# The num group of each retention step runs one step later, beside the den group, with six product tiles instead of four

## The chip, the cores and the metric

The kernel runs on one core of one Trainium2 chip. The metric is the device time of one execution in microseconds; lower is better. The core has five engines that run their own instruction streams in program order and meet through semaphores: TensorE (PE, matmuls), VectorE (DVE), ScalarE (ACT), GpSimd (POOL) and SyncE (SP, which issues the DMAs here). A "launch" is the whole program: eight images, three stages, one after the other.

## The reference

Only the first layer matters for this change. For each of 8 images with 1024 tokens of 256 channels, group-normalised, it computes, for 8 heads of 32 channels:

```
qr = theta_shift(xf @ Wq.T);  kr = theta_shift(xf @ Wk.T * SCALING);  vr = xf @ Wv.T
qk  = einsum('bhqd,bhkd->bhqk', qr, kr) * mask
den = clip(abs(qk).sum(-1), 1.0, 50000.0)
out = einsum('bhqk,bhkd->bhqd', qk / den, vr)
out = gelu(layernorm_per_head(out) * ln_g + ln_b) @ Wo.T;   x = x + out
```

There is no softmax: the weights are the scores times a fixed decay mask, divided by the sum of their absolute values. The kernel sums `num` = products times values and `den` = absolute products times ones apart, and divides later, inside the normalisation. The second layer (causal attention over 1024 tokens, then eight dense experts) follows in two more stages and is not touched.

## The kernel before

**Tiling.** The retention stage (`layer0`) walks each image `b` in 4 phases `p` of 8 steps `kt`, 32 steps in all. A phase is one group of four heads (`g = p // 2`) and one half of the 512 queries (`c = p % 2`); a step is one tile of 128 keys. The first and the last image are written out, the six between them are one loop body (`Fori(1, B - 1)`).

**A step.** Four heads make two pairs `j`. In step `i` TensorE issues, in this order: `scores` of pair 0 of the *next* step into the two-bank PSUM tile `scores0`; the first half of that step's odd job; `scores` of pair 1 of the next step into `scores1`; the second half of the odd job; the **den** group (`sums`) of step `i - 1`; the **num** group (`weighted`) of step `i`. VectorE's `products` multiplies each pair's scores by the mask window (`window`) into one of the `prod` tiles, and so frees the scores bank; ScalarE's `absolutes` takes the absolute value of each `prod` tile into one of four `absp` tiles. `scores` of pair `j` of step `i + 1` waits until `products` of pair `j` of step `i` is done, because there is just one scores tile for each pair. `prod[n % 4]` may be written again when num and the absolute value of two steps before are done.

**Odd jobs.** Between the scores pairs TensorE also does, at fixed steps: the projections for the phases to come (`q` at kt 0, `k` at kt 3, or 5 and 6 in phase 2, `v` at kt 6, or 7 in phase 2) into `bankA`; the transposes of the finished phase, `nT` (`transpose_n`, L285, into `bankB`) and `dT` (`transpose_d`, L291, into `bankA`), both at kt 1; in phase 2 the two tiny group sums `gn1` and `gn2` of the next image (L280, kt 2 and 3); `zT` and the output projections. All jobs in `bankA` stand in the list `A_MID`; each waits (`a_free`) until the one before it has been read. `dT` follows `q`, so it waits until `q` has been read by VectorE's `q_rotate_in` (L464, kt 1). `gn1` follows `dT`, so it waits for VectorE's `take_den` (L510, at kt 3 between the two products).

**Turning the phase.** After the last step of a phase ScalarE copies the sums out: `take_num` (L683, `l_tA<-l_num`) and `take_den` (L687, `l_tB<-l_den`). In step kt 0 of the new phase ScalarE's order is `take_num`, the two `absolutes`, `take_den`.

**The chain through `t1`.** A q or k that was projected is rotated in one set of buffers, `t1`, `t2`, `hi` and `lo`. In phase 3 of each image but the last, k of the next image is still in them: at kt 0, as the last thing of the step, ScalarE makes `hi` of it (`high`, L666), then GpSimd makes `lo` (`low`, L779), and only then may VectorE's `q_rotate_in` (L464) write `t1` again. VectorE runs in order, so `shuffle` (L472), `rotate_sin` (L477) and all products behind it wait with it.

Of the kernel before, what the change touches and what calls it, by code (L numbers as in the profile page):

```python
# [14 lines left out]
ACT = mybir.ActivationFunctionType  # L15
# [5 lines left out]
def layer0(nc, x, xT, wqT, wkT, wvT, woT, lng, lnb, window, rowscale, cosT, sinT, avg8, ident, x1):  # L21
# [7 lines left out]
    B, L, E = x.shape  # L29
    H, HD = 8, E // 8  # L30
    QC = 512
    KT = L // 128
# [3 lines left out]
    LN_EPS, GN_EPS = 1e-5, 1e-5  # L36
    SCALING = float(HD) ** -0.5
    STACK = 12 * 16


    A_HEAD = ["gn1", "gn2", "k", "v", "q", "v'", "k'"]
# [27 lines left out]
    with ExitStack() as ctx:  # L69
# [16 lines left out]
        kst = [sb(f"kst{g}", [128, 4, L], F32R) for g in range(2)]  # L86
        qst = [sb(f"qst{c}", [128, 4, QC], F32R) for c in range(2)]
        vsb = [sb(f"v{g}", [128, KT, 128]) for g in range(2)]
        prod = [sb(f"prod{n}", [128, 2, QC]) for n in range(4)]
        absp = [sb(f"absp{n}", [128, 2, QC]) for n in range(4)]  # L90
        tA, tB = sb("tA", [128, 4, 128]), sb("tB", [128, 4, 128])
        z = sb("z", [128, 2, L])
# [128 lines left out]
        def _(pe):  # L221
# [107 lines left out]
            def weighted(b, i, first):  # L329

                p, kt = i // KT, i % KT
                g = p // 2
                if p % 2 == 0 and kt % 4 == 0:
                    pe.wait_ge(v_ready, 4 * b + 2 * g + kt // 4 + 1)
                if kt == 0 and not (first and p == 0):
                    pe.wait_ge(n_taken, 4 * b + p)
                pe.wait_ge(prod_ready, 2 * STEPS * b + 2 * i + 2)
                for h in range(4):
                    mm = nc.tensor.matmul(num[32 * h:32 * h + 32, :], vsb[g][:, kt, 32 * h:32 * h + 32],  # L339
                                          prod[2 * (i % 2) + h // 2][:, h % 2, :], start=(kt == 0), stop=(kt == KT - 1))  # L340
                mm.then_inc(av_done, 1)

            def sums(b, i, first):
# [27 lines left out]
            def body(b, first, last):  # L371


                def A(name, task, *args):

                    if task not in (project, project_v) or args[-1] != 1:
                        a_free(name, b, first, last)
                    task(*args)

                def Bk(name, task, *args):  # L380
                    if task is not out_proj or args[-1] != 1:
                        b_free(name, b, first, last)
                    task(*args)

                for i in range(STEPS):
                    p, kt = i // KT, i % KT
                    prev = p == 0
                    post = not (prev and first)
                    tag = "3'" if prev else str(p - 1)
                    ph = nphase(b, p - 1, prev)  # L390
                    g, c = ((p + 1) // 2 % 2, (p + 1) % 2)
                    prep_q, prep_kv = p < 3 or not last, p < 2 or not last
                    nb, ni = (b, i + 1) if i + 1 < STEPS else (b + 1, 0)
                    more = i + 1 < STEPS or not last

                    def tasks(part):

                        if kt == 0 and prep_q:
                            A(f"q{p}", project, wq, g, c, part)
                        if part == 0 and kt == 1 and post:  # L400
                            Bk("nT" + tag, transpose_n, ph)
                        if part == 1 and kt == 1 and post:
                            A("dT" + tag, transpose_d, ph)
                        if part == 1 and p == 2 and kt == 2 and not last:
                            A("gn1", group_sums, mv[:, :, 0], agg_done, b + 2)
                        if part == 1 and p == 2 and kt == 3 and not last:
                            A("gn2", group_sums, gvar[:], gvar_ready, b + 2)
                        if p != 2 and kt == 3 and prep_kv:
                            A(f"k{p}", project, wk, (1 - p // 2), p % 2, part)
                        if p == 2 and kt == 5 + (1 - part) and prep_kv:  # L410
                            pe.wait_ge(xn_ready, 2 * b + 3 + (1 - part))
                            A(f"k{p}", project, wk, (1 - p // 2), p % 2, 1 - part)
                        if part == 0 and kt == 6 and post:
                            Bk("zT" + tag, transpose_z, ph)
                        if kt == 7 and p == 3:
                            Bk("o0", out_proj, 0, 0, 4 * b + 3, part)
                        if kt == 7 and prev and not first:
                            Bk("o2'", out_proj, 1, 0, 4 * b, part)
                        if kt == 4 and p == 0 and not first:
                            Bk("o1'", out_proj, 0, 1, 4 * b - 1, part)  # L420
                        if kt == 4 and p == 1 and not first:
                            Bk("o3'", out_proj, 1, 1, 4 * b, part)
                        if kt == (7 if p == 2 else 6) and prep_kv:
                            A(f"v{p}", project_v, (1 - p // 2), p % 2, part)

                    if more:
                        scores(nb, ni, 0)
                    tasks(0)
                    if more:
                        scores(nb, ni, 1)  # L430
                    tasks(1)
                    if i > 0:
                        sums(b, i - 1, first)
                    elif not first:
                        sums(b - 1, STEPS - 1, False)
                    weighted(b, i, first)

            body(0, True, False)
            with pe.Fori(1, B - 1) as b:
                body(b, False, False)  # L440
            body(B - 1, False, True)
            sums(B - 1, STEPS - 1, False)
            b_free("nT3'", B - 1, False, "after")
            transpose_n(4 * B - 1)
            a_free("dT3'", B - 1, False, "after")
# [11 lines left out]
        def _(dve):  # L457
# [21 lines left out]
            def products(b, i, j, first):  # L479
                p, kt = i // KT, i % KT  # L480
                g, c = p // 2, p % 2
                w0 = 32 * (CROWS * c - 4 * kt + ROWS - 4)
                n = 2 * i + j
                dve.wait_ge(scores_ready, 2 * STEPS * b + n + 1)
                if not (first and i < 2):
                    dve.wait_ge(av_done, STEPS * b + i - 1)
                    dve.wait_ge(abs_ready, 2 * STEPS * b + n - 3)
                nc.vector.tensor_tensor(prod[n % 4][:], sc[j][:], win[:, 4 * g + 2 * j:4 * g + 2 * j + 2, w0:w0 + QC],  # L488
                                        ALU.mult).then_inc(prod_ready, 1)

            nT = pB[:].rearrange("p (m d) -> p m d", d=32)
# [160 lines left out]
        def _(act):  # L652
# [20 lines left out]
            def absolutes(b, i, first):  # L673
                for j in range(2):
                    n = 2 * i + j
                    act.wait_ge(prod_ready, 2 * STEPS * b + n + 1)
                    if not (first and i < 2):
                        act.wait_ge(den_done, STEPS * b + i - 1)
                    nc.scalar.activation(absp[n % 4][:], prod[n % 4][:], ACT.Abs).then_inc(abs_ready, 1)  # L679

            def take_num(phase):
                act.wait_ge(av_done, KT * (phase + 1))
# [33 lines left out]
            def body(b, first, last):  # L716
                A = lambda name: a_order(name, b, first, last)
                Bn = lambda name: b_order(name, b, first, last)
                for i in range(STEPS):
                    p, kt = i // KT, i % KT  # L720
                    prev = p == 0
                    post = not (prev and first)
                    tag = "3'" if prev else str(p - 1)
                    ph = nphase(b, p - 1, prev)
                    if kt == 0 and post:
                        take_num(ph)
                    absolutes(b, i, first)
                    if kt == 0 and post:
                        take_den(ph)
                    if kt == 3 and post:  # L730
                        squares(A("dT" + tag), ph)
                    if kt == 3 and (p < 3 or not last):
                        high(prep_order(f"q{p}", b), *before(f"q{p}", b))
                    if (p < 2 or not last):
                        if kt == (6 if p == 2 else 5):
                            k_take(prep_order(f"k{p}", b), A(f"k{p}"))
                        if kt == 7:
                            if p != 2:
                                high(prep_order(f"k{p}", b), *before(f"k{p}", b))
                            v_take(A(f"v{p}"), 1 - p // 2, p % 2, 4 * b + 3 + p)  # L740
                    if p == 3 and kt == 0 and not last:
                        high(prep_order("k2", b), *before("k2", b))
                    if kt == 6 and post:
                        g, c = (1, 1) if prev else ((p - 1) // 2, (p - 1) % 2)
                        gelu(Bn("zT" + tag), ph, g, c)
# [1189 lines left out]
```

## Time and profile before

| | |
|---|---|
| median of 3 runs | 2621.92 us (2620.39 to 2627.72) |
| the profiled execution | 2624.51 us, span 2622.4 us |
| retention stage, from its first scores to its last num | about 41 to 1103 us of the span |
| TensorE busy over the span | 96% |
| VectorE, ScalarE, GpSimd busy | 70%, 55%, 20% |
| mean granted TensorE clock | 0.984 |

The profile is of one execution. Its span, from the first to the last instruction, is 2.1 us shorter than its device time, and its device time is 2.6 us above the median. Stage one is the only one in which an instruction changes place. A row of a timeline gives start, duration, engine, line, operation, tiles and what the engine's idle time before it ended with; `MATMUL` rows count two instructions for each matmul in plain float32.

### The profile page before, as it was taken

To read this page: it belongs to the slowest core of one execution; us is meant where nothing else is said; L and a number is where in the kernel's file an instruction comes from. 1 tells how busy PE (TensorE), PEld (TensorE's weight loads), DVE (VectorE), ACT (ScalarE), POOL (GpSimd) and SP (SyncE) were. 2 spreads that over 40 slices of the span, in tenths; PEclk is the share of its full clock that TensorE was granted. 3 is DMA by queue.
4 is the path that set the end of the run, shared out by engine and by line. 5 is a ranking of instruction groups with operands and counts; after the bars stand their busy time and mean duration, and the time that the engine had idled before them with its cause. 6 is when DMAs were issued, how large, how long until landed. Compare 5 with 4: busy or idle time off the path is not lost. (4 is left out here: it accounts for less than half of the span.)

```text
span 2622.4 us, 43895 instructions
## 1 busy us (share of the span) xinstructions
PE 2512.7 (96%) x15328; PEld 1786.7 (68%) x15328; DVE 1834.2 (70%) x2847; ACT 1449.9 (55%) x2044; POOL 517.6 (20%) x444
## 2 busy tenths in 40 slices
PE   5999999999999999979999969999999999999999
PEld 2444444444444444369999958888888888888888
DVE  4878777777777777657777757666666666666665
ACT  2666565566566566636566545555555555555554
POOL 2333333333333333201212110000000000000000
PEclk8999999999999999989999979999999999999999
DMA  6232222222232222123223143000000000000000
GB/s 233 51 85 60 77 62 79 65 72 75 56 85 59 83 59 70 49 71 111 82 77 115 49 146 106 18 24 24 18 23 24 24 24 24 24 24 24 24 17 16
DMA packets 116786, 157.95 MB, mean 60 GB/s; under 512 B 16272, under 2 KB 82328, under 8 KB 116384
## 3 DMA queue, kind: packets, MB, share of 16 engines
q1 hardware_dynamic: 116640, 156.01, 20.1%
q8 instruction: 91, 1.49, 0.3%
q14 instruction: 55, 0.45, 0.1%
HBM read 72.03 MB, written 33.59 MB: 40 GB/s over the span
## 5 line engine op out<-in xcount | busy, mean ns | idle before, releaser
L488 DVE TENSOR_TENSOR l_prod<-l_scores,l_window 128x1024 f32<-128x1024 f32 x512 | 615.6, 1218 | 220.7 <-PE l_scores L325 186.0
L679 ACT ACTIVATE l_absp<-l_prod 128x1024 f32<-128x1024 f32 x512 | 521.9, 1053 | 282.8 <-PE l_den L350 233.6
L1696 ACT ACTIVATE e_r<-e_h,e_bn,e_rs 128x512 f32<-128x512 f32 x512 | 399.4, 781 | 485.7 <-PE e_h L1547 484.5
L325 PE MATMUL l_scores<-l_qst,l_kst 96*128 96x512 f32 x1024 | 369.3, 457 | 27.9 <-DMA l_qst<-l_lo 12.0
L325 PEld LDWEIGHTS l_scores<-l_qst,l_kst 96*128 96x128 f32 x1024 | 167.4, 190 | 288.3 <-issue 147.9
L1547 PE MATMUL e_y<-e_whi,e_h2lo 128*128 128x256 f32 x1024 | 289.8, 283 | 0.0
L1546 PE MATMUL e_y<-e_wlo,e_h2hi 128*128 128x256 f32 x1024 | 289.7, 283 | 0.0
L1545 PE MATMUL e_y<-e_whi,e_h2hi 128*128 128x256 f32 x1024 | 289.2, 282 | 0.1
L350 PE MATMUL l_den<-l_absp,l_ones 128*32 128x512 f32 x2048 | 274.7, 609 | 0.0
L339 PE MATMUL l_num<-l_prod,l_v 128*32 128x512 f32 x2048 | 269.3, 598 | 0.0
L1791 DVE CAST e_h1hi<-e_r 128x512 fp32r<-128x512 f32 x256 | 111.2, 434 | 224.3 <-ACT e_r L1696 220.2
L1862 POOL TENSOR_TENSOR e_res<-e_res,e_bias 128x1024 f32<-128x1024 f32 x16 | 41.4, 2590 | 930.8 <-DMA e_res<-t_scratch 930.8
L1807 DVE TENSOR_TENSOR e_h2lo<-e_r,e_h2hi 128x512 fp32r<-128x512 f32 x256 | 202.3, 804 | 8.3
L1545 PE MATMUL e_h<-e_xhi,e_whi 128*128 128x512 f32 x512 | 203.0, 397 | 5.0 <-DVE e_wlo L1735 5.0
L1546 PE MATMUL e_h<-e_xlo,e_whi 128*128 128x512 f32 x512 | 202.7, 396 | 0.0
L1547 PE MATMUL e_h<-e_xhi,e_wlo 128*128 128x512 f32 x512 | 200.9, 392 | 0.0
L1545 PEld LDWEIGHTS e_y<-e_whi,e_h2hi 128*128 128x128 f32 x1024 | 196.0, 191 | 5.3 <-DVE e_h2lo L1807 0.3
L1546 PEld LDWEIGHTS e_y<-e_wlo,e_h2hi 128*128 128x128 f32 x1024 | 196.0, 191 | 5.0
L1546 PE MATMUL e_h<-e_h1lo,e_whi 128*128 128x512 f32 x512 | 199.2, 389 | 0.0
L1545 PE MATMUL e_h<-e_h1hi,e_whi 128*128 128x512 f32 x512 | 199.2, 389 | 0.0
L1547 PE MATMUL e_h<-e_h1hi,e_wlo 128*128 128x512 f32 x512 | 199.2, 389 | 0.0
L1547 PEld LDWEIGHTS e_y<-e_whi,e_h2lo 128*128 128x128 f32 x1024 | 196.1, 191 | 0.0
(191 smaller groups left out, 4472.2 us busy)
## 6 DMA issues: line engine op xcount, KB each, us to landing
l_kst<-l_hi SPq DMA_DIRECT2D x256, 64.0 KB, 2.0
l_qst<-l_hi SPq DMA_DIRECT2D x256, 64.0 KB, 2.0
l_raw<-in_xT SPq DMA_DIRECT2D x8, 1024.0 KB, 5.6
l_kst<-l_lo SPq DMA_DIRECT2D x128, 64.0 KB, 2.0
l_qst<-l_lo SPq DMA_DIRECT2D x128, 64.0 KB, 2.0
l_xo<-in_x SPq DMA_DIRECT2D x32, 256.0 KB, 2.8
x_scratch<-l_xo SPq DMA_DIRECT2D x32, 256.0 KB, 2.3
l_xr<-x_scratch SPq DMA_DIRECT2D x8, 1024.0 KB, 8.0
```

Of the source, the lines that this page charges most:

```text
L325: mm = nc.tensor.matmul(sc[j][:, s, :], kst[g][0:96, h, 128 * kt:128 * kt + 128], qst[c][0:96, h, :], start=True, stop=True)
L339: mm = nc.tensor.matmul(num[32 * h:32 * h + 32, :], vsb[g][:, kt, 32 * h:32 * h + 32], prod[2 * (i % 2) + h // 2][:, h % 2, :], start=(kt ...
L350: mm = nc.tensor.matmul(den[32 * h:32 * h + 32, :], ones[:], absp[2 * (i % 2) + h // 2][:, h % 2, :], start=(kt == 0), stop=(kt == KT - 1))
L488: nc.vector.tensor_tensor(prod[n % 4][:], sc[j][:], win[:, 4 * g + 2 * j:4 * g + 2 * j + 2, w0:w0 + QC], ALU.mult).then_inc(prod_ready, 1)
L679: nc.scalar.activation(absp[n % 4][:], prod[n % 4][:], ACT.Abs).then_inc(abs_ready, 1)
L1545: nc.tensor.matmul(o, a[0], b[0], start=start, stop=False, skip_group_check=True)
L1546: nc.tensor.matmul(o, a[0], b[1], start=False, stop=False, skip_group_check=True)
L1547: return nc.tensor.matmul(o, a[1], b[0], start=False, stop=stop, skip_group_check=True)
L1696: nc.scalar.activation(r[m][:], p[m][:], ACT.Relu, bias=bn_[layer][1][:, m, e:e + 1], scale=rs[layer][:, m, e:e + 1]).then_inc(done, 1)
L1791: nc.vector.tensor_copy(h1hi[u % 2][:, m, :], r1[m][:]).then_inc(hi1_ready, 1)
L1807: nc.vector.tensor_tensor(h2lo[u % 2][:, m, :], r2[m][:], h2hi[u % 2][:, m, :].bitcast(F32), ALU.subtract).then_inc(lo2_ready, 1)
L1862: nc.gpsimd.tensor_tensor(flat(res[c][:]), flat(res[c][:]), flat(bias[c][:]), ALU.add).then_inc(biased[c], 1)
```

## The change

The num group of step `i` moves from the end of step `i` to the end of step `i + 1`, behind the den group of the same step `i`. Since products then live a step longer, their ring grows from four to six tiles, and `products` waits for the reader of three steps before instead of two. The transposes `nT` and `dT` move from kt 1 to kt 2. ScalarE's `take_num` moves from ahead of the two `absolutes` of kt 0 to behind `take_den`. At the end of the stage one num group follows the last den group. A scratch area for DMAs that GpSimd would issue is made smaller to give room; the program has no such DMA.

```
-        prod = [sb(f"prod{n}", [128, 2, QC]) for n in range(4)]
+        prod = [sb(f"prod{n}", [128, 2, QC]) for n in range(PRODS)]
...
-                                          prod[2 * (i % 2) + h // 2][:, h % 2, :], start=(kt == 0), stop=(kt == KT - 1))
+                                          prod[(2 * i + h // 2) % PRODS][:, h % 2, :], start=(kt == 0), stop=(kt == KT - 1))
...
-                        if part == 0 and kt == 1 and post:
+                        if part == 0 and kt == 2 and post:
                             Bk("nT" + tag, transpose_n, ph)
-                        if part == 1 and kt == 1 and post:
+                        if part == 1 and kt == 2 and post:
                             A("dT" + tag, transpose_d, ph)
...
                     if i > 0:
                         sums(b, i - 1, first)
+                        weighted(b, i - 1, first)
                     elif not first:
                         sums(b - 1, STEPS - 1, False)
-                    weighted(b, i, first)
+                        weighted(b - 1, STEPS - 1, False)
...
             sums(B - 1, STEPS - 1, False)
+            weighted(B - 1, STEPS - 1, False)
...
-                if not (first and i < 2):
-                    dve.wait_ge(av_done, STEPS * b + i - 1)
-                    dve.wait_ge(abs_ready, 2 * STEPS * b + n - 3)
+                if n >= PRODS:
+                    dve.wait_ge(av_done, STEPS * b + (n - PRODS) // 2 + 1)
+                    dve.wait_ge(abs_ready, 2 * STEPS * b + n - PRODS + 1)
+                elif not first:
+                    user = 2 * STEPS - 1 - (2 * STEPS - 1 - n) % PRODS
+                    dve.wait_ge(av_done, STEPS * (b - 1) + user // 2 + 1)
+                    dve.wait_ge(abs_ready, 2 * STEPS * (b - 1) + user + 1)
...
-                    if kt == 0 and post:
-                        take_num(ph)
                     absolutes(b, i, first)
                     if kt == 0 and post:
                         take_den(ph)
+                        take_num(ph)
...
-    nc = bacc.Bacc("TRN2", target_bir_lowering=False, num_devices=1)
+    nc = bacc.Bacc("TRN2", target_bir_lowering=False, num_devices=1, dynamic_dma_scratch_size=1024)
```

The first place to look at is ScalarE in kt 0 of phase 3 (here in the first image). `l_tA<-l_num` is `take_num`, `l_tB<-l_den` is `take_den`, `l_hi<-l_t` is `high` of the next image's k; `av_done` counts num groups, `den_done` den groups. Before:

```order
L683 ACTIVATE l_tA<-l_num 128x512 [waits l0_av_done]
L679 ACTIVATE l_absp<-l_prod 128x1024 [waits l0_den_done,l0_prod_ready] x2
L687 ACTIVATE l_tB<-l_den 128x512 [waits l0_den_done]
L666 ACTIVATE l_hi<-l_t 128x512 [waits l0_sum_ready,l0_q_stacked]
L679 ACTIVATE l_absp<-l_prod 128x1024 [waits l0_den_done,l0_prod_ready] x6
```

Of the change, where ScalarE's line numbers are larger by 7:

```order
L686 ACTIVATE l_absp<-l_prod 128x1024 [waits l0_den_done,l0_prod_ready] x2
L694 ACTIVATE l_tB<-l_den 128x512 [waits l0_den_done]
L690 ACTIVATE l_tA<-l_num 128x512 [waits l0_av_done]
L673 ACTIVATE l_hi<-l_t 128x512 [waits l0_sum_ready,l0_q_stacked]
L686 ACTIVATE l_absp<-l_prod 128x1024 [waits l0_den_done,l0_prod_ready] x6
```

`take_num` now stands between `take_den` and `high`.

The second place is TensorE in kt 1 and kt 2 of phase 3. `l_bankB<-l_ident,l_tA` is `nT`, `l_bankA<-l_ident,l_tB` is `dT`. Before, kt 1 with both transposes, then kt 2:

```order
L325 MATMUL l_scores<-l_qst,l_kst 128x512 x2
L285 MATMUL l_bankB<-l_ident,l_tA 128x128 x4
L325 MATMUL l_scores<-l_qst,l_kst 128x512 x2
L291 MATMUL l_bankA<-l_ident,l_tB 128x128 x4
L350 MATMUL l_den<-l_absp,l_ones 32x512 x4
L339 MATMUL l_num<-l_prod,l_v 32x512 x4
L325 MATMUL l_scores<-l_qst,l_kst 128x512 x4
L350 MATMUL l_den<-l_absp,l_ones 32x512 x4
L339 MATMUL l_num<-l_prod,l_v 32x512 x4
```

Of the change, the same two steps:

```order
L326 MATMUL l_scores<-l_qst,l_kst 128x512 x4
L351 MATMUL l_den<-l_absp,l_ones 32x512 x4
L340 MATMUL l_num<-l_prod,l_v 32x512 x4
L326 MATMUL l_scores<-l_qst,l_kst 128x512 x2
L286 MATMUL l_bankB<-l_ident,l_tA 128x128 x4
L326 MATMUL l_scores<-l_qst,l_kst 128x512 x2
L292 MATMUL l_bankA<-l_ident,l_tB 128x128 x4
L351 MATMUL l_den<-l_absp,l_ones 32x512 x4
L340 MATMUL l_num<-l_prod,l_v 32x512 x4
```

kt 1 has lost both transposes and kt 2 has them. The order of scores, den and num within a step reads the same, but the num in it now belongs to the step before.

## Rows read from the trace of the kernel before

**Rows 1.** The page, busy time of TensorE over the whole span.

```profile
PE 2512.7 (96%) x15328; PEld 1786.7 (68%) x15328; DVE 1834.2 (70%) x2847; ACT 1449.9 (55%) x2044; POOL 517.6 (20%) x444
```

**Rows 2.** Busy times of the retention stage: span, PE, PEld, DVE, ACT, POOL, granted clock, DMA.

```profile
41.00:1103.00 1062.00, 1030.31 (x6468) 472.97 (x6472) 817.12 (x970) 653.37 (x759) 386.20 (x346) 0.99 0.27 72
```

**Rows 3.** Waits between 300 and 970 us (five images): total, times, longest.

```profile
PEld l_num L339 <- DVE l_prod L488: 7.5, 25, 0.3
...
DVE l_t L464 <- POOL l_lo L779: 16.6, 5, 3.3
...
PEld l_bankA L291 <- DVE l_t L464: 7.4, 5, 1.5
```

**Rows 4.** Timeline of TensorE, image 3, phase 3: end of kt 0 to start of kt 3.

```profile
548.71 1.04 PE L339 MATMUL l_num<-l_prod,l_v 128*32 128x512 f32 x8
549.68 0.73 PE L325 MATMUL l_scores<-l_qst,l_kst 96*128 96x512 f32 x2
550.25 0.60 PE L285 MATMUL l_bankB<-l_ident,l_tA 128*128 128x128 f32 x4
550.61 0.71 PE L325 MATMUL l_scores<-l_qst,l_kst 96*128 96x512 f32 x2
552.37 0.66 PE L291 MATMUL l_bankA<-l_ident,l_tB 128*128 128x128 f32 x4 [1.05 <-DVE l_t L464]
552.95 1.06 PE L350 MATMUL l_den<-l_absp,l_ones 128*32 128x512 f32 x8
553.84 1.04 PE L339 MATMUL l_num<-l_prod,l_v 128*32 128x512 f32 x8
554.81 1.19 PE L325 MATMUL l_scores<-l_qst,l_kst 96*128 96x512 f32 x4
555.93 1.07 PE L350 MATMUL l_den<-l_absp,l_ones 128*32 128x512 f32 x8
...
557.78 0.73 PE L325 MATMUL l_scores<-l_qst,l_kst 96*128 96x512 f32 x2
```

**Rows 5.** Timeline of VectorE in the same stretch, kt 1 and kt 2.

```profile
551.62 0.69 DVE L464 TENSOR_TENSOR l_t<-l_bankA,l_rowscale 128x512 f32<-128x512 f32 x1 [3.32 <-POOL l_lo L779]
552.23 1.22 DVE L488 TENSOR_TENSOR l_prod<-l_scores,l_window 128x1024 f32<-128x1024 f32 x1
...
553.37 0.75 DVE L472 STREAM_SHUFFLE l_t<-l_t 128x512 f32<-128x512 f32 x1
554.00 1.22 DVE L488 TENSOR_TENSOR l_prod<-l_scores,l_window 128x1024 f32<-128x1024 f32 x1
...
555.96 1.21 DVE L488 TENSOR_TENSOR l_prod<-l_scores,l_window 128x1024 f32<-128x1024 f32 x1
```

**Rows 6.** Timelines of ScalarE and GpSimd in the same stretch.

```profile
545.11 0.60 ACT L683 ACTIVATE l_tA<-l_num 128x512 f32<-128x512 f32 x1 [1.29 <-PE l_num L339]
...
548.96 0.60 ACT L687 ACTIVATE l_tB<-l_den 128x512 f32<-128x512 f32 x1 [1.36 <-PE l_den L350]
549.45 0.62 ACT L666 ACTIVATE l_hi<-l_t 128x512 fp32r<-128x512 f32 x1
...
550.22 1.28 POOL L779 TENSOR_TENSOR l_lo<-l_t,l_hi 128x512 fp32r<-128x512 f32 x1 [7.79 <-ACT l_hi L666]
```

**Rows 7.** Timeline of TensorE, image 3, phase 2, kt 2 with gn1.

```profile
521.58 0.38 PE L280 MATMUL l_bankA<-l_mv,l_avg 128*128 128x2 f32 x2 [1.18 <-DVE l_den_t L510]
521.89 1.70 PE L350 MATMUL l_den<-l_absp,l_ones 128*32 128x512 f32 x8
...
525.22 1.35 PE L325 MATMUL l_scores<-l_qst,l_kst 96*128 96x512 f32 x4
```

**Rows 8.** Busy times and granted clock after gn1 of images 1 and 3.

```profile
249.20:252.50 3.30, 3.30 (x26) 1.48 (x24) 2.59 (x8) 2.31 (x3) 0.00 (x0) 1.00 0.00 0
...
522.20:525.60 3.40, 3.40 (x17) 0.81 (x10) 2.12 (x6) 1.97 (x3) 0.00 (x0) 0.50 0.00 0
```

**Rows 9.** Timelines of TensorE and ScalarE at the stage's end.

```profile
1103.14 1.04 PE L350 MATMUL l_den<-l_absp,l_ones 128*32 128x512 f32 x8
1104.13 0.64 PE L285 MATMUL l_bankB<-l_ident,l_tA 128*128 128x128 f32 x4
...
1103.39 0.60 ACT L683 ACTIVATE l_tA<-l_num 128x512 f32<-128x512 f32 x1 [2.57 <-PE l_num L339]
```

More of the change, by code:

```diff
@@ L38, in layer0 @@
     STACK = 12 * 16
+    PRODS = 6
     A_HEAD = ["gn1", "gn2", "k", "v", "q", "v'", "k'"]
@@ L484, in products @@
                 dve.wait_ge(scores_ready, 2 * STEPS * b + n + 1)
-                if not (first and i < 2):
-                    dve.wait_ge(av_done, STEPS * b + i - 1)
-                    dve.wait_ge(abs_ready, 2 * STEPS * b + n - 3)
-                nc.vector.tensor_tensor(prod[n % 4][:], sc[j][:], win[:, 4 * g + 2 * j:4 * g + 2 * j + 2, w0:w0 + QC],
+                if n >= PRODS:
[5 more added lines that the diff above has]
+                    dve.wait_ge(abs_ready, 2 * STEPS * (b - 1) + user + 1)
+                nc.vector.tensor_tensor(prod[n % PRODS][:], sc[j][:], win[:, 4 * g + 2 * j:4 * g + 2 * j + 2, w0:w0 + QC],
                                         ALU.mult).then_inc(prod_ready, 1)
@@ L678, in absolutes @@
                         act.wait_ge(den_done, STEPS * b + i - 1)
-                    nc.scalar.activation(absp[n % 4][:], prod[n % 4][:], ACT.Abs).then_inc(abs_ready, 1)
+                    nc.scalar.activation(absp[n % 4][:], prod[n % PRODS][:], ACT.Abs).then_inc(abs_ready, 1)
             def take_num(phase):
```

## The prediction, on record before the changed kernel ran

> **What bounds the kernel now.** I read the page first: TensorE is busy for 96% of the span [rows 1]. Then the retention stage by itself: 1030 of 1062 us with a matmul in flight, VectorE 817, ScalarE 653, at a granted clock of 0.99 [rows 2]. So TensorE's own work sets the time of this stage, and no more than some 32 us of it are holes. The change removes no matmul, so only holes can be won, and any new one is a loss.
>
> Which holes? The change lets num run one step later, so the first question is whether num ever waits for its product. The waits say hardly: over five images, 160 num groups, 7.5 us in 25 waits of at most 0.3 us, and those are waits of the weight loads, which run ahead of the matmuls [rows 3]. The timeline shows why. A step without odd jobs is scores, den, num: 554.81, 555.93, 556.81, next step 557.78, that is 2.97 us without a hole [rows 4]. The product that num takes was made during the step before. The groups of den and num follow each other at 0.88 and 0.97 us whatever step they belong to. **So the delay of num itself is worth nothing**, and what remains are the things that move with it.
>
> **The change part by part.**
>
> *The ring of six and its waits: 0.* Products wait for a reader of three steps ago instead of two. num is later by one step, the ring longer by one step; the absolute value, which did not move, gets one step more. VectorE has 817 us of work in 1062, so this cover is large outside the place below. If the ring were too short, VectorE would wait about a step, 2.97 us.
>
> *The transposes from kt 1 to kt 2: 0 in most phases.* nT costs 0.36 us (550.25 to 550.61) and dT 0.58 (552.37 to 552.95) [rows 4]: kt 1 shrinks from 3.9 to 2.97 us, kt 2 grows to 3.9. VectorE needs 552.23 to 555.96 = 3.73 us for the two products, the shuffle and the sine of kt 2 [rows 5], so the longer kt 2 still covers it. Bounds: 0 to 0.1 us each in the 23 other phases that transpose.
>
> *take_num behind take_den: this is where I expect the loss.* In kt 0 of phase 3 ScalarE has `take_den` at 548.96 and, 0.49 us later, at 549.45, `high` of the next k; GpSimd's `low` starts at 550.22 and ends at 551.50 [rows 6]; VectorE's `q_rotate_in`, idle for 3.32 us until then, starts at 551.62 [rows 5]. This is a chain with no slack: each link starts within 0.15 us of the one before. Now `take_num` stands between `take_den` and `high`, and waits for the *last* num group of the phase, which has itself moved to the end of kt 0: with TensorE as before, that group runs from 548.71 to 549.75 [rows 4]. After the end of a num group take_num starts 0.07 us later (544.00 + 1.04 gave 545.04, then 545.11; the second is in [rows 6]), so at 549.82. With its 0.60 us, overlapped by 0.09 as take_den's is, `high` starts at 550.33: **0.88 us later** than before. `low` then ends at 552.38, q_rotate_in starts at 552.50, and VectorE's sequence follows with its old spacing: product of kt 2 pair 0 at 553.11 to 554.33, shuffle, product of pair 1 at 554.88 to 556.10.
>
> TensorE meanwhile: kt 1 starts at 549.68 and has nothing to wait for: its next scores 0.57 later, den at 550.80, num at 551.68, kt 2 at 552.65. There scores of kt 3, pair 0, need the product of kt 2, pair 0: 554.38 with 0.05 us for the signal, a hole of **1.73 us**. nT at 554.95; scores of pair 1 would be ready at 555.31 and need the product that ends at 556.10: start 556.15, a hole of **0.84 us**. Then dT, 556.70 (0.55 behind the scores, as den is in a plain step); den, 557.28; num 558.16; kt 3 at 559.13. Before it was 557.78 [rows 4]. TensorE loses about **1.3 us**, although dT's own old wait, 552.37 instead of 551.16 = 1.2 us, is gone and is already counted in this. Nothing gives it back later, since TensorE is the bound: the k projection, VectorE's products of kt 3 (from 556.85, ending 558.07) and the rest shift with it. Bounds: without the 0.88 us the same walk has holes of 0.85 and 0.84 us and ends at 558.25, a loss of 0.5; if VectorE were ready in time, a gain of 1.2.
>
> It happens in every image that prepares another, seven times: 7 x 1.3 = **+9.1 us** (bounds +3.5 and -8.4). In the other phases `high` isn't in kt 0, and take_num's delay meets nothing: absolute values of kt 1 come up to 0.9 us later and are wanted by a den group two scores pairs and 3 us away.
>
> *gn1: 0.* In phase 2 gn1 waits at kt 2 for take_den, 1.18 us idle [rows 7]. The dT ahead of it now lies in kt 2 as well, but take_den's time is set by VectorE, whose kt 2 was full already. Bounds per image 0 and -0.12; 0.
>
> *The end of the stage.* nT waits there for take_num, which waits for num. Before, num ended ahead of the last den group (take_num 1103.39, nT 1104.13) [rows 9]. Now den (0.88) comes ahead of num: num starts at 1104.02, ends 1105.06, take_num ends 1105.73, nT starts at about 1105.87: **+1.7 us**. The first step, which now has no num group, gives nothing back, since its successors wait for keys that a DMA brings.
>
> *The clock.* In the image of [rows 7] the hole ahead of gn1 was followed by a stretch at half clock, 1.2 instead of 2.4 GHz: granted 0.50, against 1.00 after the same hole in image 1 [rows 8]. den and num took 521.89 to 525.22 = 3.33 us instead of 1.85 [rows 4, 7]: 1.48 us a stretch. I found it after gn1 in three of seven images, never after the one hole of 1.05 us in phase 3. Now phase 3 has two holes of 1.73 and 0.84 us within one step, more idle time than at gn1. I take it in two images of seven, 2 x 1.48 = **+3.0 us** (bounds: 4 stretches fewer in all, -6, and 10 more, +15).
>
> The Trainium skill ("TensorE: Matmul & The Clock Gate", the section "Why this matters for your kernels") sees a danger for the clock only in idle gaps longer than these between bursts of matmuls. By that page the last term would be 0 and the forecast 2633. The trace of before disagrees: it shows half clock after an idle 1.18 us.
>
> **Sum.** 9.1 + 1.7 + 3.0 = 13.8 us on the profiled execution's 2624.51, that is 2638.3. This execution is 2.6 us above the median; on the median 2621.92 the same sum gives 2635.7, forecast **2636 us** (+0.5%).
>
> **The rivals.**
>
> *No difference that can be told.* A measurement of this kernel tells about 0.3%, 7.9 us. If `high` isn't delayed (ScalarE reaches take_num with num long done, because TensorE's kt 0 is earlier than I think), only the 0.5 us in phase 3 remain: 7 x 0.5 + 1.7 = 5.2, **2627**. Fewer half-clock stretches than before with the full delay end nearby (10.8 - 6 = 4.8). Against it: the links of the chain have no slack in the trace, and num's last group cannot end before 549.75.
>
> *Faster.* One mechanism: the stall no longer reaches TensorE. dT waited 1.2 us for q_rotate_in and stood ahead of den and num; now den and num pass first. It decides at the product of kt 2, pair 0: if that ended by 552.65, the step would run without a hole. It needs q_rotate_in at 550.8, 0.8 us earlier than before and 1.7 earlier than I compute. Then -8.4 + 1.7, and with the holes the three half-clock stretches might go, -4.4: -11.1, **2611**. For it: the wait at dT is real, 7.4 us in five images, 5 x 1.5 [rows 3]. Against it: VectorE's own stall, 3.3 us at its longest, 16.6 in five images [rows 3], isn't touched by moving TensorE's jobs, and the next two scores pairs depend on VectorE.
>
> *The clock makes it worse.* Every image gets a half-clock stretch in phase 3 and at gn1: up to ten more, 10.8 + 14.8 = 25.6, **2648**. For it: two holes close together. Against: in [rows 8] the same hole went either way, and holes that a low clock would fill partly are no loss.
>
> **How the numbers follow.** Main case (2628 to 2641) 0.66; the clock case (2641 to 2650) 0.12; no difference (2621 to 2629) 0.14; faster 0.08. The range 2624 to 2648 leaves out the faster case, a part of the one beside it, and the far end of the clock case, under 0.2 in all. Faster by over 0.3% (below 2614) 0.08; slower by over 0.3% (above 2629.8) 0.75, which is the main and the clock case less a little at the lower edge of the first; within 0.3% the remaining 0.17.
>
> **What would show it.** In the changed profile: q_rotate_in's idle time ahead of it about 4.2 us instead of 3.3; `high` after take_num instead of take_den; in phase 3 no wait at dT, but two waits of scores for products in kt 2, 1.7 and 0.8 us; kt 1 to kt 3 of that phase 9.4 us instead of 8.1; all other phases as long as before. The prediction is wrong if q_rotate_in starts no later relative to kt 1, if VectorE waits for num or absolute values anywhere, or if the time of other phases moves.

## The result, and the profile after

The change made the kernel slower by 1.5%: 2663.73 us median of 4 runs (2660.35 to 2667.11) against 2623.28 us (2620.39 to 2627.72) of the kernel before, ratio 1.0153, 95% interval 1.0138 to 1.0167. The forecast was 2636 us with a range up to 2648: the direction was right, the size was a third of what came, and the measured time lies outside the range. The profiled execution took 2660.35 us, its span 2658.3 us.

The page and the row of busy times of the retention stage, beside [rows 1, 2]:

```profile
PE 2527.4 (95%) x15328; PEld 1792.0 (67%) x15328; DVE 1831.2 (69%) x2847; ACT 1455.7 (55%) x2044; POOL 516.9 (19%) x444
```

```profile
41.00:1143.00 1102.00, 1048.37 (x6476) 480.12 (x6476) 814.64 (x970) 659.60 (x760) 385.67 (x346) 0.98 0.26 70
```

The stage, 1062 us long before, is 1102 us long. All 40 us are here. VectorE, ScalarE and GpSimd have as much work as before. TensorE is busy 18 us longer with as many matmuls of the same shapes, at a lower granted clock (0.98 for 0.99), and has 22 us more of holes.

The waits of five images (315 to 1019 us), to compare with [rows 3]:

```profile
PEld l_num L340 <- DVE l_prod L495: 1.8, 6, 0.3
...
PE l_scores L326 <- DVE l_prod L495: 33.1, 30, 2.3
...
DVE l_t L467 <- POOL l_lo L785: 20.9, 5, 4.2
...
DVE l_prod L495 <- PE l_num L340: 51.2, 9, 6.2
```

The first row was 7.5 us: num hardly waited for products, and now less. The third was 16.6 us, 3.3 at the longest: the stall of phase 3, grown by 0.9 us an image. The last had no counterpart: VectorE now waits for **num groups**, nine times in five images, up to 6.2 us. The prediction named this wait among the things that would make it wrong.

**Where: phase 3 first.** Timelines of TensorE, VectorE, ScalarE and GpSimd, image 3, kt 1 to kt 3, to compare with [rows 4 to 6]:

```profile
561.87 1.20 PE L326 MATMUL l_scores<-l_qst,l_kst 96*128 96x512 f32 x4
...
563.89 1.04 PE L340 MATMUL l_num<-l_prod,l_v 128*32 128x512 f32 x8
566.55 0.73 PE L326 MATMUL l_scores<-l_qst,l_kst 96*128 96x512 f32 x2 [1.62 <-DVE l_prod L495]
567.12 0.60 PE L286 MATMUL l_bankB<-l_ident,l_tA 128*128 128x128 f32 x4
568.31 1.22 PE L326 MATMUL l_scores<-l_qst,l_kst 96*128 96x512 f32 x2 [0.59 <-DVE l_prod L495]
...
573.88 1.05 PE L326 MATMUL l_scores<-l_qst,l_kst 96*128 96x512 f32 x2
...
564.68 0.69 DVE L467 TENSOR_TENSOR l_t<-l_bankA,l_rowscale 128x512 f32<-128x512 f32 x1 [4.18 <-POOL l_lo L785]
...
561.15 0.60 ACT L694 ACTIVATE l_tB<-l_den 128x512 f32<-128x512 f32 x1 [2.70 <-PE l_den L351]
562.01 0.60 ACT L690 ACTIVATE l_tA<-l_num 128x512 f32<-128x512 f32 x1 [0.26 <-PE l_num L340]
562.50 0.62 ACT L673 ACTIVATE l_hi<-l_t 128x512 fp32r<-128x512 f32 x1
...
563.27 1.29 POOL L785 TENSOR_TENSOR l_lo<-l_t,l_hi 128x512 fp32r<-128x512 f32 x1 [8.66 <-ACT l_hi L673]
```

This is the walk of the prediction, link by link. take_num starts 0.07 us after the end of num (563.89 is the next num; the last of the phase ended at 561.94). `high` starts 1.35 us behind the start of take_den, 0.49 before. q_rotate_in waits 4.18 us. The two holes stand where they were computed: by the starts, the scores of the two pairs come 1.69 and 0.83 us later than in a step without a wait (computed: 1.73 and 0.84). In an image in which the clock stayed up (image 5), kt 1, kt 2 and kt 3 together take 14.09 us against 12.79 before: +1.30, as forecast.

**And then the seam between two images.** TensorE and VectorE from kt 7 of image 3 to kt 2 of image 4:

```profile
593.82 1.04 PE L340 MATMUL l_num<-l_prod,l_v 128*32 128x512 f32 x8
597.17 0.73 PE L326 MATMUL l_scores<-l_qst,l_kst 96*128 96x512 f32 x2 [2.31 <-DVE l_prod L495]
...
602.51 1.03 PE L340 MATMUL l_num<-l_prod,l_v 128*32 128x512 f32 x8
604.99 0.73 PE L326 MATMUL l_scores<-l_qst,l_kst 96*128 96x512 f32 x2 [1.45 <-DVE l_prod L495]
606.12 0.73 PE L326 MATMUL l_scores<-l_qst,l_kst 96*128 96x512 f32 x2 [0.40 <-DVE l_prod L495]
...
595.03 2.35 DVE L495 TENSOR_TENSOR l_prod<-l_scores,l_window 128x1024 f32<-128x1024 f32 x2 [6.14 <-PE l_num L340]
...
603.71 2.36 DVE L495 TENSOR_TENSOR l_prod<-l_scores,l_window 128x1024 f32<-128x1024 f32 x2 [5.72 <-PE l_num L340]
```

Before, the same seam looked like this:

```profile
577.42 1.04 PE L339 MATMUL l_num<-l_prod,l_v 128*32 128x512 f32 x8
581.14 0.72 PE L325 MATMUL l_scores<-l_qst,l_kst 96*128 96x512 f32 x2 [2.68 <-issue]
...
585.85 0.73 PE L325 MATMUL l_scores<-l_qst,l_kst 96*128 96x512 f32 x2
...
581.99 2.47 DVE L488 TENSOR_TENSOR l_prod<-l_scores,l_window 128x1024 f32<-128x1024 f32 x2 [4.30 <-PE l_scores L325]
```

VectorE waited for scores there, and TensorE's idle 2.68 us are the turn of the loop. In the changed kernel the products of kt 0 of the new image start at 595.03, 0.17 us after the num group that ends kt 7 (593.82 + 1.04 = 594.86). Those of kt 1 start at 603.71, 0.17 us after the num group of kt 0 (603.54). The scores behind them wait, and the den and num behind those: VectorE and TensorE take turns for two steps. Nowhere else in an image does this happen: all nine waits for num of the row above stand at a seam.

The reason stands in the diff. An image has 64 products, and 64 is not a multiple of 6. Within an image product n takes tile n % 6 and follows the reader of three steps ago. But each image starts again at tile 0, whose last user is product 60, in step 30: only four products, two steps, back (`user = 63 - (63 - n) % 6` gives 60, 61, 62, 63 for n = 0 to 3). **At the seam the ring of six is a ring of four, while num is a step later.**

**The clock.** Granted clock in the stretches behind the holes of image 3 and behind the seam:

```profile
567.80:574.60 6.80, 6.29 (x24) 2.59 (x25) 4.90 (x7) 3.34 (x4) 1.98 (x2) 0.50 0.49 136
598.50:601.90 3.40, 3.40 (x9) 1.20 (x11) 0.00 (x0) 0.00 (x0) 0.00 (x0) 0.50 0.39 96
```

Both are at 1.2 GHz. Counting the first as two, since it is twice as long as the others, twelve such stretches stand in the stage of this execution: six in phase 3 (in four images) and six at the seams. In that of before there are four, three behind gn1 and one behind a turn of the loop. Left out here and in all later counts are the first 6 to 9 us of the stage, which are at half clock in every kernel.

**How the 40 us add up**, from the starts of TensorE's steps in both profiled executions, with the clock up:

| | each | times | us |
|---|---|---|---|
| phase 3, kt 1 to kt 3 | +1.30 | 7 | +9.1 |
| seam, kt 0 (6.2 for 4.70 us) and kt 1 (3.65 for 2.98) | +2.17 | 7 | +15.2 |
| seam, kt 7 (6.25 for 4.73), where no loop turn hides it | +1.5 | 2 | +3.0 |
| phase 2 with gn1 (32.53 for 32.68 us) | -0.15 | 7 | -1.0 |
| phases 0 and 1 of the images in between (32.24 for 32.16 us in phase 1) | +0.08 | 12 | +1.0 |
| half-clock stretches, sum of what they add to their steps: 18.7 for 6.3 | | | +12.4 |
| sum | | | +39.7 |

The last num of the stage ends 39.5 us later than before. What follows it is longer too:

```profile
1140.91 1.04 PE L351 MATMUL l_den<-l_absp,l_ones 128*32 128x512 f32 x8
...
1143.62 0.63 PE L286 MATMUL l_bankB<-l_ident,l_tA 128*128 128x128 f32 x4 [0.81 <-ACT l_tA L690]
```

From the last den to nT it takes 2.71 us, before 0.99 [rows 9]: +1.72, where 1.7 was forecast. At the five seams at which the loop turns, the first 1.5 us fall into the turn, which takes TensorE 2.0 to 2.8 us anyway.

### The profile page after: what moved, and what is told of

Its sections match the earlier page's. It is cut to its first block and busy times, and to the rows that moved or that the text cites. A ratio compares the mean times of both kernels' runs of the same rounds, so it can differ in the third digit from the quotient of the medians.

```text
span 2658.3 us, 43899 instructions
## 1 busy us (share of the span) xinstructions
PE 2527.4 (95%) x15328; PEld 1792.0 (67%) x15328; DVE 1831.2 (69%) x2847; ACT 1455.7 (55%) x2044; POOL 516.9 (19%) x444
## 5 line engine op out<-in xcount | busy, mean ns | idle before, releaser
L326 PE MATMUL l_scores<-l_qst,l_kst 96*128 96x512 f32 x1024 | 378.3, 465 | 58.0 <-DVE l_prod L495 45.4
```

Of the source, the lines that this page charges most:

```text
L326: mm = nc.tensor.matmul(sc[j][:, s, :], kst[g][0:96, h, 128 * kt:128 * kt + 128], qst[c][0:96, h, :], start=True, stop=True)
```

## The experiments

Line numbers are those of the kernel in question. Ratios are to the kernel before on the same chip.

**1. Eight product tiles.** 64 is a multiple of 8, so the seam is like any other step.

```
-    PRODS = 6
+    PRODS = 8
```

> The changed kernel with eight product tiles instead of six. Theory S (the seam between images): an image has 64 products, 64 is no multiple of 6, so at each of the seven seams the ring of six is in effect four long while num is a step later; products of kt 0 wait for a num group of the step before. The trace of the change shows 1.5 us more in kt 7 or in the loop's turn, 1.5 in kt 0 and 0.7 in kt 1 at each seam, 7 x 3.7 = 26 us, and some stretches at half clock beside them, 1.5 us each. Eight divides 64, so all of it goes: 2632 us (2626 to 2637), and kt 0 of phase 0 takes 4.7 us again. Rival R1, num's lag or the later take_num costs in every phase: 2655 to 2662. Rival R2, VectorE's waits on computed counts at the start of an image are slow whatever the ring: 2655 or more, kt 0 stays at 6.2 us.

Measured: 2629.11 us (2625.26 to 2633.79), before 2620.92, ratio 1.0038 (1.0025 to 1.0050). Timelines at the same seam:

```profile
581.85 0.73 PE L326 MATMUL l_scores<-l_qst,l_kst 96*128 96x512 f32 x2 [2.14 <-issue]
...
586.54 1.20 PE L326 MATMUL l_scores<-l_qst,l_kst 96*128 96x512 f32 x4
...
582.79 2.46 DVE L495 TENSOR_TENSOR l_prod<-l_scores,l_window 128x1024 f32<-128x1024 f32 x2 [3.85 <-PE l_scores L326]
```

kt 0 takes 4.69 us again, and VectorE waits for scores, as before, not for num. Against the kernel before beside it the change lost 40.4 us; with two more tiles it loses 8.2. So 32 us are gone. 18.2 are the holes of the table; the rest goes with the half-clock stretches, of which two are left in the profiled execution instead of twelve, both behind a turn of the loop. R1 and R2 are out. What stays, 8.2 us, is near what the prediction computed for everything but the clock, 10.8 us, once 3 us are taken off for the two half-clock stretches that this execution has fewer than the one before.

**2. `high` ahead of take_num**, with the ring of six. In phase 3, kt 0:

```
                         take_den(ph)
+                    if p == 3 and kt == 0 and not last:
+                        high(prep_order("k2", b), *before("k2", b))
+                    if kt == 0 and post:
                         take_num(ph)
...
-                    if p == 3 and kt == 0 and not last:
-                        high(prep_order("k2", b), *before("k2", b))
```

> The changed kernel with ScalarE's high of the next k in phase 3 between take_den and take_num, where the kernel before had it behind take_den. Theory P (the stall of phase 3): VectorE's q_rotate_in starts 0.88 us earlier again, idle 3.3 instead of 4.2 us; phase 3 loses 0.5 us to the kernel before instead of 1.3, so 7 x 0.85 = 6 us less, and fewer half-clock stretches in phase 3 (four to six of them now, 1.5 us each): 2650 us (2646 to 2659). Rival: the stall is what costs the whole 40 us: 2625. Rival: take_num's place costs nothing, 2664.

Measured: 2646.32 us (2643.87 to 2654.60), ratio 1.0092 (1.0075 to 1.0109). VectorE, then TensorE, in image 3:

```profile
561.97 0.69 DVE L467 TENSOR_TENSOR l_t<-l_bankA,l_rowscale 128x512 f32<-128x512 f32 x1 [3.33 <-POOL l_lo L786]
...
563.85 0.73 PE L326 MATMUL l_scores<-l_qst,l_kst 96*128 96x512 f32 x2 [0.77 <-DVE l_prod L495]
...
565.62 0.82 PE L326 MATMUL l_scores<-l_qst,l_kst 96*128 96x512 f32 x2 [0.60 <-DVE l_prod L495]
...
567.22 1.93 PE L351 MATMUL l_den<-l_absp,l_ones 128*32 128x512 f32 x8
```

The wait is 3.33 us as before, and kt 1 takes 3.83 us instead of 4.68, the 0.85 us that were expected. Against the kernel before beside it the loss fell from 40.4 to 25.4 us, by 15, where 7 x 0.85 = 6 are accounted for. Fewer half-clock stretches can be the rest; the profiled execution, the slowest of the four, has eleven of them, four in phase 3, and doesn't show it, so this part stays open. Den at 567.22 is in one of them: it takes 1.71 us to the start of num instead of 0.88.

**3. Both.**

> Both mends together: eight product tiles, and high between take_den and take_num. If the seam and the stall explain the change, what is left is 7 x 0.5 us in phase 3 and 1.7 us at the end, less the half-clock stretches at gn1 that the moved dT prevents: 2626 us (2620 to 2631), not to be told from the kernel before. If a third cause is at work, it stays clearly above, 2635 or more.

Measured: 2626.84 us (2623.11 to 2627.60, 10 runs), before 2620.92, ratio 1.0020 (1.0010 to 1.0029). No third cause: +5.9 us, of which 7 x 0.5 and 1.7 were computed. The interval tells it from the kernel before, which was not expected, but not by much. The 0.85 us of each image (3.83 us again for kt 1) don't show in the distance to experiment 1, 2.3 us with intervals that overlap: the profiled execution of this one has five half-clock stretches, that one's has two.

**4. The ring of six and its waits alone** (and the smaller scratch area), all else as before:

> The kernel before with the ring of six and its waits alone: num, the transposes and take_num stand where they stood before. The ring is in effect four long at the seam, but num is not late there. Theory S: 2623 us, no difference, since the four-tile ring of before is enough for num in its old place. Rival R2 (slow waits on computed counts, or the shifted place of the tiles in memory): some of the 26 us of the seams stays, 2635 to 2650.

Measured: 2620.24 us (2615.96 to 2625.50, 10 runs), ratio 0.9999 (0.9989 to 1.0008). The computed waits, the shifted memory and the four-long seam cost nothing as long as num isn't late. **Neither the ring nor the lag alone makes the seam; the two together do.** The lag with a ring of four throughout gives no time, because it cannot run: in phase 2 `gn1` waits for `take_den`, which stands behind a product of kt 3; that product waits for the num group of kt 1, and this stands behind `gn1` on TensorE.

**5. take_num behind take_den alone**, in the kernel before:

```
-                    if kt == 0 and post:
-                        take_num(ph)
                     absolutes(b, i, first)
                     if kt == 0 and post:
                         take_den(ph)
+                        take_num(ph)
```

> The kernel before with take_num behind take_den alone; num, ring and transposes as before. num is not late here, so take_num need not wait, and delays high of phase 3 by its own 0.5 us instead of 0.88. dT still stands in kt 1 and waits that much longer for q_rotate_in: kt 1 of phase 3 takes 5.6 us instead of 5.13, 7 x 0.5 = 3.5 us, 2624 us (2620 to 2628). If the order on ScalarE costs nothing, 2621.

Measured: 2659.07 us (2657.96 to 2660.53), before 2622.15, ratio 1.0140 (1.0125 to 1.0155). The expectation was wrong by ten times. TensorE and ScalarE in kt 0 of image 3, phase 1:

```profile
495.49 1.06 PE L350 MATMUL l_den<-l_absp,l_ones 128*32 128x512 f32 x8
497.76 1.06 PE L339 MATMUL l_num<-l_prod,l_v 128*32 128x512 f32 x8 [1.21 <-ACT l_tA L683]
...
497.12 0.59 ACT L683 ACTIVATE l_tA<-l_num 128x512 f32<-128x512 f32 x1
```

Without the lag the first num group of the new phase comes in kt 0 itself and overwrites the bank that take_num has yet to copy. It starts 2.27 us after den instead of 0.88, of which 1.21 are idle time in the profile, and kt 0 takes 6.1 to 6.3 us instead of 4.7. In the 23 phases 0, 1 and 2 that follow another phase this costs 1.4 to 1.6 us each. In phase 3 dT's old wait hides a part: kt 1 takes 4.21 us instead of 5.13, and the two steps together lose 0.5 us, the size that was expected for this phase. 23 x 1.45 + 7 x 0.5 + 1.4 in phase 3 of the last image are 38 us, less one half-clock stretch (three for four): 37 us. So this isn't a part that can be costed alone: the later take_num needs the later num. In the changed kernel this wait is absent (num follows den at 0.88 us).

**6. The transposes in kt 2 alone**, in the kernel before:

> The kernel before with the transposes in kt 2 alone. By the walk behind the prediction phase 3 loses 0.4 to 0.5 us (3.8 and 4.7 us for kt 1 and kt 2, instead of 5.13 and 2.98), the other phases 0 to 0.1, and gn1 is no longer followed by a stretch at half clock, because dT fills a part of its hole: 7 x 0.45 + 1.5 less 0 to 4.5 us: 2622 us (2618 to 2626). Rival, moving dT away from the wait for q_rotate_in gains its 1.2 us per image: 2612.

Measured: 2626.61 us (2624.08 to 2629.75, 10 runs), ratio 1.0019 (1.0010 to 1.0028). kt 1 and kt 2 of phase 3 take 3.82 and 4.71 us, kt 2 with gn1 5.27 us (5.02 in the first image), at full clock in all seven images. The walk was right and the rival is out; the median lies 0.6 us past the upper end of what was expected. In the profiled execution four half-clock stretches stand elsewhere, all behind the loop's turn.

**7. `high` as the first thing of kt 0 in phase 3**, in the kernel before:

```
+                    if p == 3 and kt == 0 and not last:
+                        high(prep_order("k2", b), *before("k2", b))
                     if kt == 0 and post:
                         take_num(ph)
                     absolutes(b, i, first)
...
-                    if p == 3 and kt == 0 and not last:
-                        high(prep_order("k2", b), *before("k2", b))
```

> The kernel before with ScalarE's high of the next k as the first thing of kt 0 in phase 3, ahead of take_num and the absolute values. The chain through t1 then starts some 4 us earlier, and q_rotate_in finds lo ready: kt 1 of phase 3 takes 3.86 us like those of the other phases instead of 5.13, 7 x 1.27 = 8.9 us: 2612 us (2608 to 2616). If the chain is held by something ahead of high (the q stack's DMAs), no difference: 2621.

Measured: 2616.28 us (2608.59 to 2622.26, 12 runs), before 2622.15, ratio 0.9974 (0.9963 to 0.9985). The stall is gone: kt 1 of phase 3 takes 3.86 us in all seven images, 8.9 us less work time. But the executions spread over 14 us, and the profiled one took 2622.12. Its granted clock in four stretches:

```profile
440.85:444.20 3.35, 3.35 (x6) 1.33 (x4) 2.25 (x2) 0.00 (x0) 0.00 (x0) 0.50 0.33 79
519.40:522.70 3.30, 3.30 (x17) 0.88 (x10) 2.02 (x6) 2.04 (x3) 0.00 (x0) 0.50 0.00 0
577.40:580.70 3.30, 3.30 (x6) 1.34 (x4) 2.17 (x2) 0.00 (x0) 0.00 (x0) 0.50 0.36 87
655.90:659.20 3.30, 3.30 (x17) 0.81 (x10) 2.07 (x6) 1.96 (x3) 0.00 (x0) 0.50 0.00 0
```

Half clock behind gn1 and behind the turn of the loop, at the same two places in image after image, ten stretches in all, six more than before: 6 x 1.5 = 9 us, as much as the mend had given. Over the twelve executions the time goes with the mean granted clock of the whole program: 0.985 at 2608.59 us, 0.981 at 2622.26.

**8. The change with both causes removed**: eight tiles, and `high` first. It was measured twice, the second time beside experiment 9.

> The changed kernel with eight product tiles and high as the first thing of kt 0 in phase 3: no seam, no stall. kt 1 and kt 2 of phase 3 take 2.98 and 3.9 us like those of the other phases, 7 x 1.7 us less than with high between take_den and take_num (2626.8): 2615 us (2611 to 2619). If num's later place is worth nothing, as the prediction had it, this is not below the kernel before with the same move of high (2612 expected); if the lag is worth something once its costs are gone, it is below that.

> The same kernel as a_ring8_hi_top, beside the one above on the same chip: 2613 us (2610 to 2617), for the comparison of the two.

Measured: 2613.33 us (2611.80 to 2615.53), before 2622.15, ratio 0.9965 (0.9952 to 0.9978); and 2611.22 us (2606.07 to 2612.99), before 2622.39, ratio 0.9954 (0.9942 to 0.9966). Both are as expected, and kt 1 and kt 2 of phase 3 take 2.98 and 3.95 us.

**9. No lag, the transposes in kt 2, `high` first**:

> The kernel before with high first in phase 3 and the transposes in kt 2; num, ring and take_num as before. No stall in phase 3 (kt 1 and kt 2 2.98 and 3.95 us), and no half-clock stretch at gn1, where dT fills part of the hole, so none of the stretches that ate a part of the gain of moving high alone (2616): 2612 us (2608 to 2616), 1 to 2 us under the changed kernel with the same mends (2613), which has one num group more behind the last step. If num's lag is worth something of its own, that one is the faster.

Measured: 2606.61 us (2602.85 to 2611.51), before 2622.39, ratio **0.9948** (0.9935 to 0.9961). It is below what was expected. Its retention stage, to its last num at 1086.8 us:

```profile
41.00:1093.00 1052.00, 1029.51 (x6492) 475.99 (x6492) 818.39 (x975) 657.50 (x762) 388.29 (x350) 1.00 0.27 73
```

Behind its first 9 us no stretch of the stage is at half clock in this execution, the fastest of the five. With the lag and eight tiles the median is 4.6 us higher, 2611.22, but the two intervals overlap, so the medians hardly tell them apart; 1.7 of the 4.6 would be the longer end of the stage, and two half-clock stretches stand in its profiled execution. The steps at full clock tell more: phases 0, 1 and 2 take 33.97, 32.24 and 32.54 us here and 33.99, 32.24 and 32.55 us with the lag, phase 3 ahead of the last image 32.26 and 32.22. So the lag of num, with all its costs repaired, is worth nothing, as the prediction had it.

## Why the prediction was right and wrong

**What bounds the kernel: right.** TensorE's own work does, and num did not wait. The lag gave nothing (experiments 8 and 9).

**take_num and the stall of phase 3: right, to 0.1 us.** Forecast +1.3 us an image, measured +1.30. Experiment 2 shows the term by itself in the steps: kt 1 takes 3.83 us instead of 4.68 once `high` is ahead of take_num.

**The transposes: right.** 0 to 0.1 us in the other phases, measured 0.08 (32.24 for 32.16 us in phase 1). gn1, forecast 0 with a bound of -0.12, gave -0.15 us an image, just past the bound.

**The ring of six: this step failed.** The prediction says: "num is later by one step, the ring longer by one step", cost 0. That holds inside an image. It took the ring's length from the number of tiles and not from the distance between two users of one tile, and never asked what happens where the count starts again, though the formula for it stood in the diff. It even named the price of a ring that is too short, "about a step, 2.97 us". The trace of the change shows 2.2 us at each seam, or 3.7 where no loop turn hides a part, and experiment 1 shows that they go when the ring fits. No rival held it either. With the ring term the same sum, 13.8 + 18.2 = 32.0 us, would have given 2654 us.

**The clock: the right mechanism, mis-sized.** I took two more half-clock stretches, 3.0 us. There were eight more, 12.4 us, six of the twelve in phase 3 and the others at the seam, which the walk did not contain. In a kernel with the stall but without the seam (experiment 1) there were two in all and none in phase 3, whose two holes were the same; why the six went with the seam is open. The section of the Trainium skill that I weighed ("TensorE: Matmul & The Clock Gate", "Why this matters for your kernels") warns of longer gaps only; the runs disagree with it again: a hole of 1.62 us and one of 0.59 us stood ahead of the stretch at 0.50 shown above.

**The end of the stage: right.** Forecast +1.7 us, measured +1.72. **The first step: right.** Forecast 0: kt 3 of the first image, which waits for keys in both kernels, starts at 56.6 us of the span, before at 57.0.

## What to carry to other kernels

A ring of buffers is as long as the shortest distance between two users of one tile. Where the index starts again at tile 0 with each turn, and the number of uses isn't a multiple of the number of tiles, the ring is shorter at that place: four instead of six here. When one engine's reader is moved later, walk the ring through the loop's seam, not only through its middle. And when an engine that is the bound gets short holes, count the clock too: a mend that removes work can be eaten by stretches at half clock that fall on the same place each time round, so judge it over several executions.

## What was not expected of the hardware

TensorE's granted clock fell to half behind short idle times, and not behind each. A hole of 1.18 us at gn1 was followed by 0.50 in three of seven images before and in five of seven in experiment 7, but in none of experiment 5. With dT moved to kt 2 this hole is at most 0.95 us, and none of those kernels shows 0.50 behind it. But holes of 0.77 and 0.60 us within one step, in phase 3 of experiment 2, were followed by it in four of seven images, and in none of experiment 6, where kt 2 of phase 3 takes the same 4.71 us. One stretch added 1.5 to 1.7 us to the steps it fell on. The executions of one kernel spread over 3 to 14 us.
